# A two-layer block on one core: guards of scale factors as scalar_tensor_tensor, new instruction lists for the first half, and another order behind the last expert

## What is computed

```python
x = x + tanh(g_xattn[0]) * xattn(layernorm(x), fside, ctx)   # per batch b
x = x + tanh(g_ffn[0]) * ffn(layernorm(x), ...)

# xattn: two quantised linears with a SiLU gate between them
s = sqrt(max(amax_x, EPS) / max(amax_w, EPS)); s = max(s, EPS)
xs, ws = x / s, w * s
x_scale = max(rowmax(abs(xs)), EPS) / 127   # w_scale likewise
out = round(xs / x_scale) @ round(ws / w_scale).T * x_scale * w_scale.T

# ffn: 16 experts of inner width 352, the best 2 for each token, capacity 256,
# and a shared expert of inner width 704 for all tokens
y = sum over the 2 of weight * (silu(h @ w_gate) * (h @ w_up)) @ w_down
y = y + (silu(h @ ws_gate) * (h @ ws_up)) @ ws_down
```

## Time and profile before

| | us |
|---|---|
| median of 3 runs (597.97 to 598.31) | 598.0 |
| the profiled execution | 599.84 |
| its span from the first to the last instruction | 598.1 |
| TensorE busy | 560.9 |
| VectorE busy | 415.8 |
| ScalarE busy | 296.1 |
| GpSimd busy | 156.9 |
| mean granted clock of TensorE, of full speed | 0.981 |

### The profile page before, as it was taken

The page is one execution under the profiler, slowest core; times in us unless marked ns, Lnnn a source line. Parts: engine busy times, 40 slices in busy tenths (PEclk is TensorE's granted clock), DMA queues, the critical chain, the costliest instruction groups (busy, mean ns, idle before and its releaser), DMA issues.

```text
span 598.1 us, 10333 instructions
## 1 busy us (share of the span) xinstructions
PE 560.9 (94%) x3949; PEld 478.8 (80%) x3949; DVE 415.8 (70%) x755; ACT 296.1 (50%) x460; POOL 156.9 (26%) x157
## 2 busy tenths in 40 slices
PE   7977989999998999999998999999999999999991
PEld 3544647988896888888887899999999999999980
DVE  4868796997899757566826766665666666666586
ACT  3175574386338541543146556556556666653110
POOL 2469510231041101010041222222232220006772
PEclk9979899999999999999999999999999999999995
DMA  7911021013001120011076667777777765755686
GB/s 261 385 48 64 13 94 71 2 36 141 1 2 37 70 98 2 1 71 50 2 243 188 216 219 239 232 261 239 248 248 231 232 215 181 231 206 154 199 279 241
DMA packets 45460, 89.01 MB, mean 149 GB/s; under 512 B 4256, under 2 KB 24736, under 8 KB 44400
## 3 DMA queue, kind: packets, MB, share of 16 engines
q1 hardware_dynamic: 40304, 71.74, 35.5%
q0 software_dynamic: 5120, 16.78, 9.2%
HBM read 71.73 MB, written 16.78 MB: 148 GB/s over the span
## 4 chain that ended last, share of the span: by engine, by line
PE 66%; DVE 14%; POOL 6%; DMA 5%; issue 4%; ACT 4%; SPq 1%; POOLq 0%; DVEq 0%; ACTq 0%
PE ps_gu L1710 12%; PE ps_gu L1711 11%; PE ps_gu L1712 11%; POOL got L554 5%; PE ps_d L1710 5%; PE ps_d L1711 5%; PE ps_d L1712 5%; PE ps_a L1938 2%; PE ps_d L1731 2%; DMA raw_d<-in_L_ffn_w_down 2%; PE ps_a L1731 2%; PE ps_a L1799 2%; DMA w<-in_ctx 2%; PE ps_gu L1752 1%; DVE xn L1119 1%
## 5 line engine op out<-in xcount | busy, mean ns | idle before, releaser
L1710 PE MATMUL ps_gu<-ex_xhi,w_hi 128*128 128x256 f32 (+1 forms) x480 | 136.9, 285 | 1.7 <-DVE w_lo L1321 1.7
L1711 PE MATMUL ps_gu<-ex_xlo,w_hi 128*128 128x256 f32 (+1 forms) x480 | 135.0, 281 | 0.0
L1712 PE MATMUL ps_gu<-ex_xhi,w_lo 128*128 128x256 f32 (+1 forms) x480 | 134.8, 281 | 0.0
L1710 PEld LDWEIGHTS ps_gu<-ex_xhi,w_hi 128*128 128x128 f32 (+1 forms) x480 | 86.3, 180 | 6.7 <-issue 5.6
L1711 PEld LDWEIGHTS ps_gu<-ex_xlo,w_hi 128*128 128x128 f32 (+1 forms) x480 | 86.1, 179 | 1.2
L1712 PEld LDWEIGHTS ps_gu<-ex_xhi,w_lo 128*128 128x128 f32 (+1 forms) x480 | 86.3, 180 | 0.0
L1710 PE MATMUL ps_gu<-xt_hi,sw_hi 128*128 128x256 f32 x264 | 78.7, 298 | 1.0 <-DVE sh_hid L1293 1.0
L1711 PE MATMUL ps_gu<-xt_lo,sw_hi 128*128 128x256 f32 x264 | 74.4, 282 | 0.0
L1712 PE MATMUL ps_gu<-xt_hi,sw_lo 128*128 128x256 f32 x264 | 74.4, 282 | 0.0
L1321 DVE TENSOR_TENSOR w_lo<-raw_gu,w_hi 128x1408 fp32r<-128x1408 f32 x36 | 58.2, 1616 | 1.1 <-DMA x2n_scratch<-y 1.1
L1710 PEld LDWEIGHTS ps_gu<-xt_hi,sw_hi 128*128 128x128 f32 x264 | 50.0, 190 | 5.4 <-DVE sh_hid L1293 1.7
(11 more groups left out here) (217 smaller groups left out, 1129.3 us busy)
## 6 DMA issues: line engine op xcount, KB each, us to landing
raw_gu<-in_L_ffn_w_gate SPq DMA_DIRECT2D x16, 704.0 KB, 4.5
raw_gu<-in_L_ffn_w_up SPq DMA_DIRECT2D x16, 704.0 KB, 6.0
raw_d<-in_L_ffn_w_down SPq DMA_DIRECT2D x16, 512.0 KB, 7.3
expert_out_scratch<-eo SPq DMA_DIRECT2D x16, 512.0 KB, 7.5
w<-in_fside_BxS2xS SPq DMA_DIRECT2D x4, 1024.0 KB, 5.2
x2n_scratch<-y SPq DMA_DIRECT2D x4, 1024.0 KB, 3.8
out<-x SPq DMA_DIRECT2D x8, 512.0 KB, 4.7
x<-in_x SPq DMA_DIRECT2D x1, 3072.0 KB, 16.7
```

The source lines that it names most:

```text
L1710: pe.matmul(dst, a_hi, b_hi, start=start, stop=False)
L1711: pe.matmul(dst, a_hi, b_lo, start=False, stop=False)
L1712: return pe.matmul(dst, a_lo, b_hi, start=False, stop=stop)
```

## The change

Four things change.

1. The three guards are no longer tensor_scalar. They are scalar_tensor_tensor instructions with the constant 1e-6 as scalar and a constant tile as second input (ones, or 1/127 in the new tile inv_qmax).
2. The lists of GpSimd, ScalarE, VectorE and TensorE for the first half, and the order of a few DMAs on SyncE, are other permutations of the same calls; the number of keep_busy matmuls goes from 157 to 135.
3. Behind the loop over the experts, down(E - 1, 1, 2) comes ahead of up(E, 0, 0) on TensorE, and rows_out(E - 1) ahead of weights_gu(E + 1) on ScalarE.
4. The slot numbers of all batches are copied at once, ahead of the wait for the last expert's store. The last batch has a semaphore for each quarter, its adds go quarter by quarter, and its output is stored in four pieces of 256 KB.

The core of the diff; the lists are cut to the stretches that the prediction speaks of:

```diff
-            load_w2(1)
             load_w1(2)
             store_x2n(0)
+            load_w2(1)
             load_w2(2)
...
+            for j in range(J):
+                sp.wait_ge(summed, 2 * (B - 1) + j + 1)
+                sp.dma_start(out_v[B - 1][:, j], x2[:, B - 1, j]).then_inc(out_done, 16)
...
 # GpSimd
             norm_a(0)
             root_a(0)
+            scale_w(0)
             norm_a(1)
-            scale_w(0)
-            norm_a(2)
             split_gu_lo(0)
-            norm_a(3)
             split_gu_lo(1)
-            split_gu_lo(2)
-            split_gu_lo(3)
-            split_d_lo(0)
             root_b(0)
-            split_d_lo(1)
             root_a(1)
             scale_w2(0)
             scale_w(1)
+            split_d_lo(0)
+            split_gu_lo(2)
             norm_b(0)
+            split_gu_lo(3)
+            norm_a(2)
+            root_b(1)
+            split_d_lo(1)
             root_a(2)
-            root_b(1)
...
+            pool.tensor_copy(slot_col[:].rearrange("p b j n -> p b n j"), slots[:]).then_inc(slot_cols, 1)
+            pool.wait_ge(slot_cols, 1)
+            pool.sem_inc(cols_staged, 1)
             pool.wait_ge(eo_out[0], 16 * (E // 2))
...
 # ScalarE, behind the integers of batch 0
+            tanh()
+            split_gu_hi(0)
+            silu_a(0)
+            split_gu_hi(1)
+            normalise_a(1)
             split_gu_hi(2)
...
             normalise_b(0)
-            silu_a(1)
             x_hi(0, 0)
             x_hi(0, 1)
-            normalise_a(2)
+            split_d_hi(1)
             x_hi(0, 2)
             x_hi(0, 3)
+            silu_a(1)
             copy_logits(0)
+            normalise_a(2)
...
             step(E - 1, E // 2 - 1, 1)
+            rows_out(E - 1, E // 2 - 1, 1)
             weights_gu(E + 1, E // 2, 1)
             hidden(E, 0, 0, False)
-            rows_out(E - 1, E // 2 - 1, 1)
...
 # VectorE
+            def at_least_eps(dst, src, factor):
+                return dve.scalar_tensor_tensor(out=dst, in0=src, scalar=Q_EPS, in1=factor, op0=ALU.max, op1=ALU.mult)
...
-                link(dve.tensor_scalar(w, sm["amax_w"][:, 0:width], Q_EPS, None, ALU.max))
+                link(at_least_eps(w, sm["amax_w"][:, 0:width], ones[:, 0:width]))
...
-                dve.tensor_scalar(smooth, small[layer]["root"][:, 0:n], Q_EPS, None, ALU.max).then_inc(ready, 1)
+                at_least_eps(smooth, small[layer]["root"][:, 0:n], ones[:, 0:n]).then_inc(ready, 1)
...
-                return dve.tensor_scalar(small[layer][which + "_step"][:], row_max, Q_EPS, 1.0 / QMAX, ALU.max, ALU.mult)
+                return at_least_eps(small[layer][which + "_step"][:], row_max, inv_qmax)
...
             ratio_a(0)
-            router()
             smooth_a(0)
-            stats_a(1)
+            amax_w2(0, 0)
             scale_x(0)
             x_steps(0)
+            stats_a(1)
+            w_steps(0)
             stats_a(2)
-            w_steps(0)
...
             scale_g(0)
+            smooth_a(1)
             g_steps(0)
-            smooth_a(1)
             w2_steps(0)
             scale_x(1)
             x_steps(1)
+            w_steps(1)
             dequant_b(0, 0)
             dequant_b(0, 1)
-            w_steps(1)
...
+            def add_last(j):
+                b, k = B - 1, (B - 1) % 3
+                dve.wait_ge(got_last[j], 32)
+                dve.scalar_tensor_tensor(out=x2[:, b, j, :], in0=got[k][:, j, 0, :], scalar=wts[:, b, 0, j:j + 1],
+                                         in1=x2[:, b, j, :], op0=ALU.mult, op1=ALU.add).then_inc(sum_half, 1)
+                dve.wait_ge(sum_half, 2 * b + j + 1)
+                dve.scalar_tensor_tensor(out=x2[:, b, j, :], in0=got[k][:, j, 1, :], scalar=wts[:, b, 1, j:j + 1],
+                                         in1=x2[:, b, j, :], op0=ALU.mult, op1=ALU.add).then_inc(summed, 1)
...
 # TensorE
-            keep_busy(29)
+            keep_busy(23)
             turn_qx(0, 0)
...
+            turn_w(2, 3)
             keep_busy(1)
-            turn_x(2, 1)
-            keep_busy(3)
             logits(0)
-            turn_x(2, 2)
             shared_up(0, 0, 0, 0)
...
             table(3)
             shared_down(2, 1, 1, 1)
-            shared_up(2, 1, 4, 0)
+            shared_up(2, 1, 5, 0)
             shared_down(2, 1, 2, 0)
-            shared_up(2, 1, 4, 1)
             shared_down(2, 1, 2, 1)
-            shared_up(2, 1, 5, 0)
             shared_down(2, 1, 3, 0)
+            shared_down(2, 1, 3, 1)
             turn_tokens(0, 0, 0)
-            shared_down(2, 1, 3, 1)
...
-                up(e, q, 0, w=w)
-                down(e - 1, 1 - q, 2, w=weights_of(e - 1))
+                if e == E:
+                    down(e - 1, 1 - q, 2, w=weights_of(e - 1))
+                    up(e, q, 0, w=w)
+                else:
+                    up(e, q, 0, w=w)
+                    down(e - 1, 1 - q, 2, w=weights_of(e - 1))
```

More of the change, by code:

```diff
@@ L260, in flamingo_block @@
         cols_staged = sem("cols_staged")
+        got_last = [sem(f"got_last{j}") for j in range(J)]
         slot_cols, got_in, sum_half, summed, out_done = (
@@ L1701, in _ @@
             dve.wait_ge(ex_eo, NE)
-            add_rows(3, 0)
-            add_rows(3, 1)
+            for j in range(J):
+                add_last(j)
         @block.tensor
@@ L2002, in _ @@
             row_s(1)
+            keep_busy(9)
             turn_qg(0)
@@ L2097, in _ @@
+            turn_y(1, 2)
+            shared_down(0, 0, 4, 1)
+            turn_y(1, 3)
+            turn_w(3, 0)
+            shared_up(0, 1, 2, 1)
+            logits(1)
+            shared_up(0, 1, 3, 0)
+            shared_down(0, 0, 5, 0)
+            turn_logits(1)
             turn_w(3, 1)
-            shared_down(0, 0, 3, 1)
-            turn_y(1, 3)
-            shared_down(0, 0, 4, 0)
+            shared_up(0, 1, 3, 1)
+            shared_down(0, 0, 5, 1)
+            rank(0)
+            shared_up(0, 1, 4, 0)
@@ L2101, in _ @@
             turn_w(3, 2)
-            shared_down(0, 0, 4, 1)
-            logits(1)
+            shared_up(0, 1, 4, 1)
+            table(0)
             turn_w(3, 3)
-            shared_down(0, 0, 5, 0)
+            turn_w2(2, 0)
             turn_x(3, 0)
-            turn_logits(1)
+            shared_up(0, 1, 5, 0)
+            shared_down(0, 1, 0, 0)
+            turn_w2(2, 1)
+            shared_down(0, 1, 0, 1)
             turn_x(3, 1)
-            rank(0)
+            turn_g(2, 0)
+            shared_down(0, 1, 1, 0)
@@ L2126, in _ @@
[L2126 removed]
+            turn_g(2, 1)
+            shared_down(0, 1, 1, 1)
+            turn_x(3, 3)
+            shared_up(1, 0, 0, 0)
+            shared_down(0, 1, 2, 0)
+            shared_up(1, 0, 0, 1)
+            shared_down(0, 1, 2, 1)
+            row_b(2)
+            shared_up(1, 0, 1, 0)
             row_rs(3)
[L2128 to L2130 removed]
+            shared_down(0, 1, 3, 0)
+            shared_up(1, 0, 1, 1)
@@ L2140, in _ @@
             turn_qw2(2)
-            shared_down(0, 1, 4, 0)
+            shared_up(1, 0, 3, 0)
+            product_b(2, 0)
+            shared_up(1, 0, 3, 1)
+            product_b(2, 1)
+            shared_down(0, 1, 5, 1)
             turn_qx(3, 0)
-            shared_down(0, 1, 4, 1)
-            product_b(2, 0)
+            shared_up(1, 0, 4, 0)
+            product_b(2, 2)
+            shared_down(1, 0, 0, 0)
             turn_qx(3, 1)
-            product_b(2, 1)
-            shared_down(0, 1, 5, 0)
@@ L2158, in _ @@
-            shared_up(1, 0, 3, 0)
+            shared_up(1, 1, 0, 0)
             product_a(3, 0)
-            shared_up(1, 0, 3, 1)
+            shared_up(1, 1, 0, 1)
             product_a(3, 1)
-            shared_up(1, 0, 4, 0)
+            turn_y(2, 0)
+            shared_down(1, 0, 2, 1)
+            turn_y(2, 1)
+            shared_down(1, 0, 3, 0)
+            turn_y(2, 2)
+            shared_up(1, 1, 1, 0)
             product_a(3, 2)
-            shared_up(1, 0, 4, 1)
-            turn_y(2, 0)
+            shared_down(1, 0, 3, 1)
@@ L2196, in _ @@
             shared_up(1, 1, 3, 1)
+            table(1)
             shared_up(1, 1, 4, 0)
-            row_b(3)
-            shared_down(1, 1, 0, 0)
-            shared_up(1, 1, 4, 1)
-            shared_down(1, 1, 0, 1)
-            shared_up(1, 1, 5, 0)
-            shared_down(1, 1, 1, 0)
-            shared_down(1, 1, 1, 1)
+            shared_down(1, 1, 0, 0)
+            turn_w2(3, 0)
+            shared_down(1, 1, 0, 1)
+            turn_w2(3, 1)
+            shared_down(1, 1, 1, 0)
+            turn_g(3, 0)
@@ L2205, in _ @@
+            shared_down(1, 1, 1, 1)
+            shared_up(1, 1, 4, 1)
+            turn_g(3, 1)
+            shared_up(1, 1, 5, 0)
+            shared_down(1, 1, 2, 0)
+            shared_up(2, 0, 0, 0)
+            row_b(3)
+            shared_up(2, 0, 0, 1)
+            shared_down(1, 1, 2, 1)
+            shared_up(2, 0, 1, 0)
+            shared_down(1, 1, 3, 0)
```

(13 more changed lines are left out.)

616 lines of the change are left out of this document (279 added, 337 removed).

## The result

| | before | after |
|---|---|---|
| median, us (20 executions each, same chips) | 598.16 | 595.94 |
| ratio, with its 95% interval | | 0.9964 (0.9955 to 0.9972) |
| the profiled execution | 599.84 | 595.79 |
| its span | 598.1 | 593.9 |
| mean granted clock | 0.981 | 0.986 |

Faster, but by 2.2 us where 5.4 were forecast, though the two profiled spans lie 4.2 us apart. So two things are to be explained: where 1.2 us of the forecast went in the trace, and why the medians show only half of what the traces show. The executions of either kernel fall into two groups: of the 20 of before, 15 lie at 597.65 to 598.61 us and five at 599.25 to 600.37; of the changed kernel's, 13 at 594.77 to 596.32 and seven at 597.00 to 598.26; the profiled execution of before lies in its upper group, that of the changed kernel in its lower.

What follows compares the result with a forecast made beforehand. TensorE was taken to carry the time: start of the dense stage, fixed matmuls, holes and tail. -7.6 +1.0 +1.2 +0.3, with the weights' -0.3, gave -5.4 us: span 592.7, median 592.6 us, range 588 to 598.5.

Steps and rivals of the forecast that it cites:

- Part 1, the guards: 32 VectorE guards rewritten as scalar_tensor_tensor still wait for GpSimd: gain 0, bounds -7.7 us and 0.
- rival of the free guards: The new guards don't wait for GpSimd; logits(0) near 85.6, 589.4 us in all; chance 0.13.
- Term 1: New lists in batch 0 start logits(0) at 88.8 instead of 97.31, two transposes still to do: -7.6 us.
- The race at 59.2 us: Batch 0: w_step_b(0) comes 0.1 us before scale_w(1); rival that it falls behind: 595.5 us, chance 0.14.
- the step from span to median: End of the sum: profiled execution 599.84 and runs' median 598.0 turn a span of 592.7 into a median of 592.6.
- Term 2: Dense stage from logits(0) on: three or four more waits for GpSimd, +1.0 us, bounds 0 and +5.
- Term 3: End of the dense stage: TensorE waits 1.7 to 2.2 us for expert 0's tokens, +1.2 us, bounds 0.5 and 3.
- Term 4: Expert 15 and tail: 1.0 us wait ahead of down(15,2), offset by gather wait and last store: +0.3 us net.
- The dense stage did not give it back: Rival: dense-stage waits come whole, five on TensorE's path instead of half hidden: 598 us; chance 0.12.
- The last batch's routing: Rival: late top_two(3) opens TensorE holes before the tokens; slower from 6.6 us lateness, 8 us gives 601; chance 0.09.

Runs made afterwards that it cites:

- the two one-part kernels: Only the guards' form changed: changed kernel with tensor_scalar guards again, ratio 0.9996; kernel before with the new guards only, 610.05 us, ratio 1.0011.
- a1_after: The changed kernel itself, unaltered, measured again on other chips against the kernel before: 610.53 us, ratio 1.0008.
- b2_tail_alone: The kernel before with only the changed tail and its tile of constants, lists of batch 0 as before: 610.79 us, ratio 1.0022.
- e1_hold: Changed kernel, but SyncE issues expert 1's weights only when the gather of expert 0's tokens has landed: 607.10 us, ratio 0.9957 to the kernel before.
- e13_all_gate: Changed kernel with expert 1's weights held for the gather, split_d_lo(0) behind norm_a(2), 12 more fillers, batch 2's gathers held until down(18,0): 596.45 us, ratio 0.9787.
- a0_after: The changed kernel itself, unaltered, measured on other chips against the kernel before: 610.39 us, ratio 1.0013.

## Why the prediction was right or wrong

- **Part 1, the guards: right.** 0 was forecast, bounds -7.7 to 0; the two one-part kernels gave 0. The rival of the free guards is dead.
- **Term 1, batch 0: right in its walk, short by 1.5 us, and with one wrong link.** logits(0) at 87.32 for 88.8. The forecast put 1 us of slow clock behind the hole ahead of row_rs(1). It is there in some executions (a1_after) and not in others. The race at 59.2 us was won (w_step_b(0) at 58.62, scale_w(1) at 58.99).
- **Its reference was wrong: the second step that failed.** Of the 3.3 us between the forecast of 592.6 and the median of 595.94, 1.2 are the spans (592.7 forecast, 593.9 measured) and 2.1 the step from span to median. The walk took from rows 3 and 4 that row_w and what follows run at the low clock, and booked their return to full clock as a gain of the change. Three profiles show the same lists without it, b2_tail_alone 1.7 us earlier. The step from a span of 592.7 to a median of 592.6 had the same flaw: the profiled execution, 599.84, lay 1.8 us above the median of its own kernel. I took those 1.8 off the forecast, as if the changed kernel had the same accident to lose. Against the undisturbed trace the same steps give 3.7 us.
- **Term 2, the dense stage: too dear.** Its waits were forecast at +1.0. Between logits(0) and the tokens +0.3 came, and that holds 0.9 of transposes and 0.7 of the moved shared_down, so that the stage itself gave 1.3 back: TensorE was idle there for 1.2 us less than before. The guards do meet GpSimd (105.57 us, 2.34), but off TensorE's path.
- **Term 3, the hand-over: the step that failed in the trace.** +1.2 was forecast, bounds 0.5 and 3, and -0.3 for the weights; 5.6 came, 4.5 of waiting and 1.1 behind it, and 6.3 for equal work. Terms 1, 2 and 4 came out 3.5 us better than forecast (1.5, 1.6 and 0.4) and hid three quarters of it. The count of cover was right: TensorE was ready at 294.7, 6.2 us behind table(3). The length of the index and the gather was taken over from before (8.3 us) as a constant, although the prediction itself noted that expert 1's weights start earlier. It booked that as a gain of 0.3 and didn't ask what they collide with. e1_hold shows it: without them the wait is 1.66, where 1.7 to 2.2 was forecast.
- **Term 4, the tail: near in the first measurement** (wait 0.92 for 1.0, no wait of the last add, -0.1 net for +0.3). On the other chips the whole changed tail costs 1.3 us; which part does, stays open.
- **The rivals.** The dense stage did not give it back. The last batch's routing was late by 0.3 us only (so long table(3) waited for VectorE), but the hole it spoke of opened all the same, from the other side of the gather: DMA, not VectorE.
- **The chances.** 0.80 on faster by over 0.2% came out, with 0.36%. The range of 588 to 598.5 held the time, but the forecast's own band of 590.5 to 595, which had 0.52, missed it by 0.9, and none of the rivals describes what happened. That the sum came within 1.2 us of the span is in part luck: errors of both signs in terms 1 to 4.

What stays open: why the standstill in the tail shows on the chips of the experiments and not in the first measurement, at the same rate of gathers (DMA share 0.74 and 0.77). That it is TensorE's own instructions that arrive late is argued, not shown: the trace names no releaser. Thirteen of the experiments' profiles have the changed order behind expert 15. In ten of them the first such wait ends 28.8 to 28.9 us behind the start of down(15,2), which fits a fixed place in the instruction stream as well as a fixed time behind the first gather. The Trainium skill (Runtime: NRT & Kernel Launch, section Instruction fetch mechanics) says that each engine's sequencer fetches its instructions by a DMA queue of its own, mostly hidden. e13_all_gate would fit a fetch that is not hidden while gathers fill the DMA engines, but the instruction packets in the traces don't bear it out. In a0_after the queue with 16 KB packets has one at 541.1 us and the next at 572.9, with 134 matmuls of TensorE between them; in the first measurement they are at 541.3 and 560.7, with 143. So the packets come with the progress of the work, and none lands at the end of the standstill (569.5). Which engine that queue serves isn't shown. The first profile and the ratio of 0.9964 belong to chips without it; on those with it the changed kernel is at 1.0008 to 1.0013. Its tail costs 1.3 us there and its two holes another 1.5 in some executions, which could take back the 2.4 of the traces; that it is these two and nothing else is not shown.

## What to carry to other kernels

When a list is shortened, look at every DMA whose release moves with it, and ask what it shares the DMA engines with: a prefetch that ScalarE first read 19 us later (311.58), released some 5 us too early, cost 4.2 us in the trace, as much as the whole change gained there, and one wait gave it back (2.5 us in the medians). Price a TensorE hole with and without the slow clock behind it, and never book a slow clock seen in one profile as something that a change removes: compare that profile's own time with the median first. Of several waits, first end those behind which the clock fell in some executions (here the ones of 2.5 and 3.0 us), with filler or by moving their cause to where nobody waits for it. And run a kernel's tail on more than one chip before pricing it.
